# Cross attention of block one: score products on two 64-row halves of PE, stacked keys re-laid for it, shifts placed by transfers

## The reference, cut to what matters

```python
B, NQ, NK, C, H = 32, 56, 1500, 128, 16;  D = C // H          # D = 8
q  = (ln(x) @ Wq + bq).reshape(B, NQ, H, D)
kv = (context @ Wkv + bkv).reshape(B, NK, 2, H, D)
k, v = kv[:, :, 0], kv[:, :, 1]
s = einsum('bqhd,bkhd->bhqk', q, k) / sqrt(D)
p = softmax(s, axis=-1)
x = x + (einsum('bhqk,bkhd->bqhd', p, v).reshape(B, NQ, C) @ Woc + boc)
```

## Time and profile before

| | |
|---|---|
| median of 3 runs | 2227.27 us (2222.23 to 2234.25) |
| profiled execution | 2220.8 us, span 2219.0 us, mean granted PE clock 0.917 |
| PE busy over the span | 1897.6 us (86%) |
| DVE, ACT, POOL busy | 67%, 63%, 43% |
| cross attention of block one | from about 430 to about 1142 us of the span |
| exponentials of it (L1235) | 384, mean 917 ns |
| score products (L1183) | 1536, mean 259 ns |

### The profile page before, as it was taken

How to read it: one execution, slowest core, us unless ns; L and a number is a source line. 1 busy time by engine, 2 the same in 40 slices (tenths; PEclk the granted TensorE clock), 3 DMA queues, 4 the chain that set the end, 5 groups by cost and what they waited for, 6 DMA issues and landing times. The chain is left out here.

```text
span 2219.0 us, 57559 instructions
## 1 busy us (share of the span) xinstructions
PE 1897.6 (86%) x19877; PEld 1284.0 (58%) x19877; DVE 1490.4 (67%) x2708; ACT 1396.4 (63%) x2431; POOL 955.3 (43%) x1151
## 2 busy tenths in 40 slices
PE   4888676789999999999988887656899999999988
PEld 3888333256666666666653555233466666666653
DVE  3688578666666666666632332697488888888883
ACT  3787233356666666666633334433799999999963
POOL 0000064244454544545400000251688888888840
PEclk9899778799999999999988889755899999999989
DMA  7788100133332333333230997000011111111100
GB/s 210 222 257 257 17 1 0 42 78 96 90 94 83 90 90 84 98 88 90 72 103 20 272 290 222 0 0 28 29 46 52 43 42 42 42 42 42 42 1 17
DMA packets 64286, 190.38 MB, mean 86 GB/s; under 512 B 19886, under 2 KB 27294, under 8 KB 64222
## 3 DMA queue, kind: packets, MB, share of 16 engines
q1 hardware_dynamic: 59614, 164.95, 26.5%
q0 software_dynamic: 4608, 24.58, 2.8%
HBM read 127.13 MB, written 25.49 MB: 69 GB/s over the span
## 5 line engine op out<-in xcount | busy, mean ns | idle before, releaser
L1289 DVE TENSOR_REDUCE c_part<-c_mxp 128x1 f32<-128x500 f32 x672 | 429.0, 678 | 207.9 <-PE c_mxp L1168 207.7
L1235 ACT ACTIVATE c_e<-c_stp 125x896 f32<-125x896 f32 x384 | 349.4, 917 | 167.6 <-PE c_stp L1183 166.4
L1936 ACT ACTIVATE c_e<-c_sp,alpha 128x750 f32<-128x750 f32 x448 | 393.0, 896 | 16.9 <-PE c_sp L1881 16.9
L1168 PE MATMUL c_mxp<-c_kh,c_qb 128*128 128x500 f16 x672 | 254.4, 381 | 11.1 <-DVE c_part L1289 6.9
L1958 DVE TENSOR_SCALAR c_pt<-c_tp 125x768 bf16<-125x768 f16 x448 | 245.6, 550 | 2.1 <-PE c_tp L1894 0.8
L1894 PE MATMUL c_tp<-ident_h,c_ph 128*128 128x128 f16 x2688 | 224.3, 220 | 19.0 <-DVE c_pt L1958 15.8
L1894 PEld LDWEIGHTS c_tp<-ident_h,c_ph 128*128 128x128 f16 x2688 | 178.0, 98 | 106.1 <-DVE c_pt L1958 60.3
L1972 DVE TENSOR_SCALAR c_ph<-c_e,c_inv 128x1500 f16<-128x1500 f32 x224 | 231.2, 1032 | 0.1
L1881 PE MATMUL c_sp<-c_ki,c_qb 128*128 128x375 bf16 x896 | 218.7, 326 | 10.5 <-ACT c_e L1936 10.0
L1183 PE MATMUL c_stp<-c_qs,c_ks 103*128 103x224 f16 x1536 | 210.2, 259 | 2.5 <-ACT c_e L1235 2.5
L1183 PEld LDWEIGHTS c_stp<-c_qs,c_ks 103*128 103x128 f16 x1536 | 147.2, 98 | 72.1 <-issue 20.5
(11 more groups left out here) (276 smaller groups left out, 3534.7 us busy)
## 6 DMA issues: line engine op xcount, KB each, us to landing
c_ct<-ctx_turned SPq DMA_DIRECT2D x64, 750.0 KB
ctx_turned<-l_ct POOLq DMA_DIRECT2D x32, 750.0 KB, 7.6
c_ks<-c_kh SPq DMA_DIRECT2D x256, 93.8 KB
f_ct<-ctx_turned SPq DMA_DIRECT2D x32, 750.0 KB
l_cn<-in_ctx SPq DMA_DIRECT2D x32, 672.0 KB
f_cn<-in_ctx SPq DMA_DIRECT2D x32, 672.0 KB
c_ks<-c_kl SPq DMA_DIRECT2D x128, 93.8 KB
l_cn<-in_ctx SPq DMA_DIRECT2D x32, 78.0 KB
```

Source lines behind the costliest of these rows:

```text
L1168: pe.matmul(mxp[:, (PIECES * p + s) % 2, 0:500], qh[p][:, 128 * (s // 3):128 * (s // 3) + 128], kh[p][:, 500 * (s % 3):500 * (s % 3) + 500 ...
L1235: act.activation(e[:, j % (2 * GROUP), :].rearrange("p (a c) -> p a c", a=2), stp[0:KP, 2 * (j % 2):2 * (j % 2) + 2, 0:448], ACT.Exp, scal ...
L1289: dve.reduce_max(part[:, s // 3, s % 3:s % 3 + 1], mxp[:, (PIECES * p + s) % 2, 0:500], axis=AX.X).then_inc(piece_max, 1)
L1936: act.activation(e[t % E_BUFFERS][:, HALF * h:HALF * h + HALF] .rearrange("p (k c) -> p k c", k=2), sp_[:, 2 * h:2 * h + 2, 0:375], ACT.Ex ...
```

## The change

- The array's rows are used as two halves of 64. Half 0 holds the key channels 0 to 63, half 1 the channels 64 to 127. `ks` is 128 rows by 4 groups: in each half, for 16 channels, rows 0 to 15 kh, 16 to 31 kh, 32 to 47 ones, 48 to 63 kl. SP fills it with 24 transfers of 16 rows by 3000 bytes instead of 12 of 32 rows. DVE sets all 128 rows of `ks` to one at the start instead of 7, and SP's first transfers wait for that.
- `qs` is 128 rows by 448 columns. A score step of a key block is eight products of 112 columns with `tile_position=(0, 0)` or `(64, 0)`, two halves by four groups, each half into its own PSUM bank, instead of four products of 224 columns.
- The shift is one row in each half (32 and 96). It is no longer laid by POOL with a mask of 7 tiles: `topt` is f16, and SP sends it to its places with 8 transfers of one row (six of 128 columns, two of 64). They stand in SP's step behind the load of the context and ahead of the transfers into `ks`. SP waits there for the spread queries and for `topt`; the first score product waits for the 8 transfers.
- POOL spreads the queries with one instruction over 128 rows by 448 columns instead of four over 96 by 224.
- In `tokens_l1_cross` the stacked queries have 128 rows; ACT multiplies by a mask column, and DVE's instruction covers all rows. One small DVE instruction makes the masked bias, and ACT waits for it at the start.
- Weights are loaded with 12 instead of 6 small transfers into `wqs` and `bqs`, which POOL sets to zero before.

```diff
-    for t in range(3):
-        loads.append((m.wqs[:, :, 32 * t:32 * t + 32], w["L1_xattn_Wq"].rearrange("c (g r) -> c g r", g=4)))
-        loads.append((m.bqs[32 * t:32 * t + 32, :], w["L1_xattn_bq"].rearrange("(g r) -> r g", g=4)))
+    for half in range(2):
+        wide, narrow = w["L1_xattn_Wq"][:, 64 * half:64 * half + 64], w["L1_xattn_bq"][64 * half:64 * half + 64]
+        for at in (0, 16, 48):
+            a = 64 * half + at
+            loads.append((m.wqs[:, :, a:a + 16], wide.rearrange("c (g r) -> c g r", g=4)))
+            loads.append((m.bqs[a:a + 16, :], narrow.rearrange("(g r) -> r g", g=4)))
...
+                dve.tensor_scalar(m.bqm[:, :], m.bqs[:, :], m.mask_rows[:, 2:3], None, ALU.mult).then_inc(small, 1)
...
-                        dve.scalar_tensor_tensor(out=m.qst[32:64, g, cols(c)], in0=bank[32:64, 4 + i % 4, 0:CH],
-                                                 scalar=m.bqs[32:64, g:g + 1], in1=m.qst[32:64, g, cols(c)],
+                        dve.scalar_tensor_tensor(out=m.qst[:, g, cols(c)], in0=bank[:, 4 + i % 4, 0:CH],
+                                                 scalar=m.bqs[:, g:g + 1], in1=m.qst[:, g, cols(c)],
                                                  op0=ALU.add, op1=ALU.subtract).then_inc(qs_low, 1)
 
...
+                act.wait_ge(small, 7)
...
-                        act.activation(m.qst[:, g, cols(c)], bank[0:96, 4 + i % 4, 0:CH], ACT.Identity,
-                                       bias=m.bqs[:, g:g + 1]).then_inc(qs_high, 1)
+                        act.activation(m.qst[:, g, cols(c)], bank[:, 4 + i % 4, 0:CH], ACT.Identity,
+                                       bias=m.bqm[:, g:g + 1], scale=m.mask_rows[:, 2:3]).then_inc(qs_high, 1)
...
-        ks = pair("ks", [96 + NT, 4, W], F16)
+        ks = pair("ks", [128, 4, W], F16)
         vx = pair("vx", [KP, NJ, 8, 32])
         qh = pair("qb", [128, HQ], F16)
-        qs = pair("qs", [96 + NT, HQ], F16)
+        qs = pair("qs", [128, HQ // 2], F16)
         e = sb("e", [KP, 2 * GROUP, HQ])
         kf = sb("kf", [128, 3, 500])
-        topt = sb("topt", [NT, 128])
+        topt = sb("topt", [NT, 128], F16)
...
+                    if live(2):
+                        sp.wait_ge(qs_spread, n - 1)
+                        sp.wait_ge(top_copied, n - 1)
+                        for t in range(NT):
+                            for c in (0, 64):
+                                at = 128 * t + c
+                                row, at = (32, at) if at < HQ // 2 else (96, at - HQ // 2)
+                                if t == NT // 2:
+                                    sp.dma_start(qs[p][row:row + 1, at:at + 64], topt[t:t + 1, c:c + 64]
+                                                 ).then_inc(shift_sent[p], 16)
+                                elif c == 0:
+                                    sp.dma_start(qs[p][row:row + 1, at:at + 128], topt[t:t + 1, :]
+                                                 ).then_inc(shift_sent[p], 16)
                     if live(1):
                         r = 1 - p
+                        if not live(2):
+                            sp.wait_ge(ones_set, 2)
                         if live(3):
                             wait_apart(sp, scored, NJ * (n - 2), beat)
                         sp.wait_ge(k_high, 3 * n)
-                        for t in range(2):
+                        for at in (0, 16):
+                            for half in (0, 64):
+                                for g in range(4):
+                                    sp.dma_start(ks[r][half + at:half + at + 16, g, 0:NK],
+                                                 kh[r][half + 16 * g:half + 16 * g + 16, 0:NK]
+                                                 ).then_inc(stacked[r], 16)
+                        sp.wait_ge(k_low, 3 * n)
+                        for half in (0, 64):
                             for g in range(4):
-                                sp.dma_start(ks[r][32 * t:32 * t + 32, g, 0:NK], kh[r][32 * g:32 * g + 32, 0:NK]
+                                sp.dma_start(ks[r][half + 48:half + 64, g, 0:NK],
+                                             kl[r][half + 16 * g:half + 16 * g + 16, 0:NK]
                                              ).then_inc(stacked[r], 16)
-                        sp.wait_ge(k_low, 3 * n)
-                        for g in range(4):
-                            sp.dma_start(ks[r][64:96, g, 0:NK], kl[r][32 * g:32 * g + 32, 0:NK]
-                                         ).then_inc(stacked[r], 16)
-                sweep(sp, step, 1)
+                sweep(sp, step, 2)
...
-                    pool.memset(ks[p][0:96, :, NK:W], 0.0).then_inc(set_once, 1)
...
-                    for g in range(4):
-                        last = pool.tensor_tensor(
-                            qs[p][0:96, 4 * NQ * g:4 * NQ * (g + 1)].rearrange("p (h q) -> p h q", h=4),
-                            m.qst[:, g, tokens(a)].rearrange("p (o q) -> p o q", o=1).to_broadcast([96, 4, NQ]),
-                            m.mask_quad[0:96, :].rearrange("p (h o) -> p h o", o=1).to_broadcast([96, 4, NQ]),
-                            ALU.mult)
-                    last.then_inc(qs_spread, 1)
+                    pool.tensor_tensor(qs[p][:, :].rearrange("p (g h q) -> p g h q", g=4, h=2),
+                                       m.qst[:, :, tokens(a)].rearrange("p g (o q) -> p g o q", o=1)
+                                       .to_broadcast([128, 4, 2, NQ]),
+                                       m.mask_rows[:, 0:2].rearrange("p (o h u) -> p o h u", o=1, u=1)
+                                       .to_broadcast([128, 4, 2, NQ]), ALU.mult).then_inc(qs_spread, 1)
...
-                def lay_shift(a, p, more):
-
-                    if more:
-                        pool.wait_ge(k_low, 3 * a + 6)
-                    pool.wait_ge(top_copied, a + 1)
-                    pool.tensor_tensor(qs[p][96:96 + NT, :].rearrange("p (t c) -> p t c", t=NT),
-                                       topt[:, :].rearrange("p (o c) -> p o c", o=1).to_broadcast([NT, NT, 128]),
-                                       m.mask_tile[:, :].rearrange("p (t o) -> p t o", o=1)
-                                       .to_broadcast([NT, NT, 128]), ALU.mult).then_inc(shift_laid, 1)
...
-                        pe.wait_ge(stacked[p], transfers(a, p, 12))
+                        pe.wait_ge(stacked[p], transfers(a, p, 24))
                         pe.wait_ge(qs_spread, a + 1)
-                        pe.wait_ge(shift_laid, a + 1)
+                        pe.wait_ge(shift_sent[p], transfers(a, p, 8))
                     if j >= 2 or not first:
                         pe.wait_ge(exped, NJ * a + j - 1)
                     for g in range(4):
-                        last = pe.matmul(stp[:, 2 * (j % 2) + g // 2, 224 * (g % 2):224 * (g % 2) + 224],
-                                         ks[p][:, g, KP * j:KP * j + 128], qs[p][:, 224 * g:224 * g + 224],
-                                         start=True, stop=True)
+                        for half in range(2):
+                            r = 64 * half
+                            last = pe.matmul(stp[:, 2 * (j % 2) + half, 112 * g:112 * g + 112],
+                                             ks[p][r:r + 64, g, KP * j:KP * j + 128],
+                                             qs[p][r:r + 64, 112 * g:112 * g + 112], start=True, stop=True,
+                                             tile_position=(r, 0))
...
-                    dve.memset(ks[p][96:96 + NT, :, :], 1.0).then_inc(ones_set, 1)
+                    dve.memset(ks[p][:, :, :], 1.0).then_inc(ones_set, 1)
...
```

More of the change, by code:

```diff
@@ L151, in weight_loads @@
                      (m.mask_head, w["mask_head"]), (m.mask_quad, w["mask_quad"]),
-                     (m.mask_triple, w["mask_triple"]), (m.mask_tile, w["mask_tile"]),
+                     (m.mask_triple, w["mask_triple"]), (m.mask_rows, w["mask_rows"]),
                      (m.mask_pair, w["mask_pair"])):
@@ L209, in _ @@
             def _(pool):
-                for t in (m.woca, m.wocb, m.bva, m.bvb):
+                for t in (m.woca, m.wocb, m.bva, m.bvb, m.bqs):
                     pool.memset(t[:, :], 0.0)
+                pool.memset(m.wqs[:, :, :], 0.0)
                 pool.memset(m.mean[:, :], 1.0 / D)
@@ L992, in _ @@
                             pe.wait_ge(qs_low, i - 3)
-                        pe.matmul(bank[0:96, 4 + i % 4, 0:CH], m.wqs[:, g, :], m.h[:, cols(c)], start=True, stop=True
+                        pe.matmul(bank[:, 4 + i % 4, 0:CH], m.wqs[:, g, :], m.h[:, cols(c)], start=True, stop=True
                                   ).then_inc(qs_done, 1)
@@ L1026, in cross_attention @@
         pp = ps("pp", [128, BANK])
-        stacked = [sem(f"stacked{p}") for p in range(2)]
+        stacked, shift_sent = ([sem(f"{s}{p}") for p in range(2)] for s in ("stacked", "shift_sent"))
```

(23 more changed lines are left out.)

3 lines of the change are left out of this document (removed).

## The result

The changed kernel takes 2305.34 us (median of 4 runs, 2304.08 to 2313.05) against 2224.75 us of the kernel before on the same chip. The ratio is 1.0364, with a 95% interval of 1.0321 to 1.0406: slower. The profiled execution has a span of 2303.8 us, 84.8 more than before, and a mean granted clock of 0.911 against 0.917.

The account below looks back on a forecast made before the run. PE's order of work bounds the stage; 31 items pay 2.18 us each, 68 us, score groups 0: 2289 us profiled, 2295 as a median, 3.1% slower. Its own range is 2275 to 2315 us, for 8 in 10 2205 to 2325.

Parts of the forecast that it names:

- PE is the bound, and a stand of PE is paid in full: In this stage PE's order of work bounds; its wait for the shift delays everything behind, 2.18 us in 31 items.
- The path: From the end of the shift's copy over eight SP issues to the last landing: 6.3 us, against a 4.12 us slot.
- the near price of an issue: Each SP transfer of the shift costs 0.62 us to issue, as on the same queue's SBUF to SBUF transfers.
- Score groups: Each of 12 groups an item takes 0.40 us with both turns against 0.39 before: nothing gained.
- Eight of twelve groups count: Even a pure gain of 0.19 us a score group would count in only eight, 1.5 us an item.
- 24 key transfers hidden: SP's 24 issues into the stacked keys take 14.9 us an item, hidden; the next context load has 1 us of cover.
- Weight loads as the bound: Rival: eight full 98 ns loads make a score group 0.98 us, 225 us in all, 2450 us; chance 0.03.
- The clock: A clock below 1.00 in the stage, from PE standing 2 us at a time, would add time not in the sum.
- The stand: PE's wait before each item's first score product: 6.3 - 4.12 = 2.18 us, 68 us over 31 items.
- The cheap issues: Rival: shift transfers cost 0.37 us to issue, path 4.5 us, halves drain; 12 us slower, 2240 us; chance 0.20.
- both rivals without a drain: Halves turn without draining PE: with dear issues 2265 us, chance 0.13; with cheap issues 2210 us, chance 0.18.

Follow-up runs that it names:

- e1: Changed kernel with the shift placed by POOL in seven rows of each half instead of by eight transfers: 2224.34 us, ratio 1.0008 to the kernel before.
- e6: Changed kernel with the shift sent in 4 transfers instead of 8: 2225.98 us, ratio 0.9994.
- e2: Kernel before with only the shift's placing changed, seven one-row transfers by SP instead of POOL's instruction: 2270.61 us, ratio 1.0220.
- e7: Changed kernel with the shift sent in 14 transfers of 64 columns instead of 8: 2470.97 us, ratio 1.1113.
- e5: e1 with the score groups of two key blocks made next to each other in every second slot: 2187.11 us, ratio 0.9845.
- e4: Kernel before with only the stacked keys' transfers changed, 24 of 16 rows instead of 12 of 32: 2219.27 us, ratio 0.9999.
- e3: Changed kernel with the first score product one slot later, slot 3 instead of 2: 2250.30 us, ratio 1.0126.

## Why the prediction was right

The forecast was 2295 us, 68 more than before; the median is 2305.34, 80.6 more. The mechanism holds, and the terms came out as follows.

- *PE is the bound, and a stand of PE is paid in full.* Right but for a little: against e1, which has no stand, an item is 23.55 - 21.63 = 1.92 us longer by a stand of 2.05 in the mean, 60 us for 31 items. Where the stands are taken away (e1, e6) the time is that of the kernel before.
- *The path.* Forecast 6.3 us by the near price of an issue; measured 6.35 in the mean of 20 items. The last landing, 1.8 us in the sum, came 1.7 us after its issue. The issue price was the open choice, 0.62 or 0.37 us. The near row, same queue and same kind, was the right one, for one row of 256 bytes as for 32 rows of 3000. With 4, 7, 8 and 14 issues (e6's last item, e2, the changed kernel, e7) it is 3.98, 5.67, 6.35 and 10.1 us, about 0.6 us for each issue more.
- *Score groups.* Forecast 0.40 against 0.39 us, measured 0.30 after a 0.10 longer way in. e5 shows the two parts. The 0.01 us a group that the forecast put at nothing are most of the 0.17 us an item, 5 us in all, by which e1 is longer than the kernel before. The Trainium skill says in "TensorEngine Tiling (Array Packing)", "Tiling Modes", that a change of the tiling mode drains the engine. The traces agree for halves of rows as for quarters of columns, with about 0.10 us each way.
- *Eight of twelve groups count.* Not tested by itself; with no gain in a group there was nothing to count.
- *24 key transfers hidden.* Right in the kernel before (e4) and, but for 0.2 us of waits for a context load, in the changed kernel; the cover is thin, as e3 shows.
- *Weight loads as the bound.* It falls: 16 loads and their products in a pair take 0.50 us with the way out, so eight loads fit into 0.20.
- *The clock.* Left out of the sum and named as what could add time. It added about 15 us. With it and the 3 us of the first and last items the 65 us of the longer item are the 83.3 us of the stage.
- *The stand.* Slightly overrated: the forecast took 6.3 - 4.12 = 2.18 us an item. But the halves had made the slot itself longer, 4.27 us in e1, so PE stood 2.05; and some waits vanish behind the stand (the keys' second product starts 0.32 us behind its piece in e1 and 0.22 here), so 1.92 came of it. That these 8 us too many and the 5 us of the score groups nearly cancel is luck.

The cheap issues fall by the 0.62 us of the changed kernel's own trace, by e6 and by e7, and both rivals without a drain by e5. What stays open is when the clock falls. The runs show that it comes with the length of PE's stand (1.5 us in the mean: 2 stretches in this stage, 2.2 us: 10, about 6 us: 30). In the changed kernel the stands are 1.7 to 1.8 us in every other item, and none of these brought a stretch; of the 17 of 2.2 us and more between the first and the last copy 10 did, and the two of e2 stand beside stands of 2.1. Why one stand of 2.3 us does and the next doesn't no run here shows.

## What to carry to other kernels

Count the issues on a path, not the bytes: a transfer from SBUF to SBUF that is tiny still holds its queue for 0.6 us here, so scattering one small result into eight places costs 5 us where one engine instruction cost 1.7. Splitting the array pays only for what is done between two turns: with one short group between whole-array products the turns ate all of it, with two groups the same split gave 1.5%. And before moving work in a schedule, check every double buffer that the moved work used to cover, not only the one whose wait is in view.

## What the runs showed of the hardware that was not expected

- The price of an issue does not fall with rows or bytes for SBUF to SBUF, as long as rows go to rows: 0.59 us for 32 x 3000, 16 x 3000, 1 x 256 and 1 x 128 bytes (medians), while a 750 KB load from DRAM takes 0.33 us of the same queue.
- A transfer that collects three rows of `topt` into one row of `qs` takes 0.7 us to issue and saves two others (e6).
- Stands of PE of 2.2 to 2.3 us are enough to bring single stretches at 1.2 GHz, each worth about 1.5 us.
